# Moving the FFN units of a fused attention and FFN layer behind the output projection, and the weight build behind the first projections

## What is computed

```python
q = (x @ Wq + bq); k = (x @ Wk + bk); v = (x @ Wv + bv)     # 16, 2, 2 heads of 64
scores = einsum('bgrsd,bgswd->bgrsw', q, k_win)             # window of 256 keys around s
out = einsum('bgrsw,bgswd->bgrsd', softmax(scores), v_win)
x = layernorm(x + out @ Wo + bo)
W_real = unfold(G1_R, G2_R); W_imag = unfold(G1_I, G2_I)    # 512 x 512 each
xr, xi = split(x, 2)
y = layernorm(x + concat(xr @ W_real.T - xi @ W_imag.T + br,
                         xr @ W_imag.T + xi @ W_real.T + bi))
```

## Time and profile before

| | us |
|---|---|
| median of 3 runs | 1383.55 |
| lowest and highest of them | 1379.75, 1401.43 |
| the profiled execution | 1378.04 |
| its span on the slowest core (7) | 1376.5 |
| spans of all cores | 1366.8 to 1376.5 |

### The profile page before, as it was taken

How to read it: one execution, slowest core, us unless ns; L and a number is a source line. 1 busy time by engine, 2 the same in 40 slices (tenths; PEclk the granted TensorE clock), 3 DMA queues, 4 the chain that set the end, 5 groups by cost and what they waited for, 6 DMA issues and landing times.

```text
span 1376.5 us, 17007 instructions; the slowest of 8 cores (1366.8 to 1376.5 us)
## 1 busy us (share of the span) xinstructions
PE 808.0 (59%) x4568; PEld 357.5 (26%) x4568; DVE 553.9 (40%) x1539; ACT 396.1 (29%) x673; POOL 356.7 (26%) x324
## 2 busy tenths in 40 slices
PE   0033377665577666666665575666577558665654
PEld 0000132322233223332232232233232223222321
DVE  0044410355514551455554011455425541555553
ACT  3311134322333223332220234233232233332310
POOL 0000002443303340334330104433214430343410
PEclk9999987777677777877777686777687768877776
DMA  4500100000100001000000310000200020000000
GB/s 132 175 11 0 62 31 0 1 16 31 63 15 16 16 32 61 17 16 16 32 16 16 107 31 1 16 16 16 77 1 17 31 77 1 16 17 31 16 16 31
DMA packets 15869, 44.51 MB, mean 32 GB/s; under 512 B 3091, under 2 KB 5539, under 8 KB 15782
## 3 DMA queue, kind: packets, MB, share of 16 engines
q0 software_dynamic: 9216, 33.56, 6.7%
q1 hardware_dynamic: 6566, 9.87, 2.6%
HBM read 26.65 MB, written 16.78 MB: 32 GB/s over the span
## 4 chain that ended last, share of the span: by engine, by line
PE 53%; DVE 21%; issue 10%; DMA 7%; ACT 5%; POOL 1%; DVEq 1%; SPq 0%; ACTq 0%; POOLq 0%
PE pW L631 11%; PE pW L758 10%; PE pW L405 9%; PE pS L556 5%; DVE scr L644 5%; PE pS L499 4%; DVE attn L584 4%; DMA xs<-x 4%; PE pT L729 2%; PE pT L606 2%; DVE pre L777 2%; DVE x_tm L709 2%; PE pW L762 2%; DVE pre L674 1%; PE pW L635 1%
## 5 line engine op out<-in xcount | busy, mean ns | idle before, releaser
L517 ACT ACTIVATE EX<-pS,expbias 128x512 bf16<-128x512 f32 x384 | 242.7, 683 | 329.5 <-PE pS L499 329.1
L533 POOL TENSOR_TENSOR EX<-EX,maskr_s 128x512 bf16<-128x512 bf16 x128 | 172.1, 1368 | 276.0 <-ACT EX L517 275.4
L533 POOL TENSOR_TENSOR EX<-EX,maskl_s 128x512 bf16<-128x512 bf16 x128 | 148.5, 1181 | 323.7 <-ACT EX L517 323.7
L631 PE MATMUL pW<-wo_sb,attnT 128*128 128x512 bf16 x512 | 174.6, 502 | 35.3 <-DVE pre L777 33.8
L405 PE MATMUL pW<-XT,wq_sb 128*128 128x512 bf16 x512 | 127.8, 416 | 9.1 <-DVE XT L385 9.1
L729 PE MATMUL pT<-identb,x_tm 128*128 128x128 bf16 x256 | 32.3, 305 | 169.8 <-DVE x_tm L709 169.8
L644 DVE SCALAR_TENSOR_TENSOR scr<-pre 128x1024 bf16<-128x1024 f32 x64 | 120.5, 1883 | 6.7
L584 DVE TENSOR_SCALAR attn<-pS,Rrec 128x64 bf16<-128x64 f32 x512 | 110.2, 278 | 14.3 <-DVE attn L584 0.5
L499 PE MATMUL pS<-QT,KT 64*128 64x512 bf16 x384 | 101.9, 473 | 13.3 <-ACT EX L517 11.5
L574 DVE RECIPROCAL Rrec<-pS 128x4 f32<-128x4 f32 x128 | 23.3, 182 | 188.2 <-PE pS L556 187.9
L556 PE MATMUL pS<-VB,EX 128*128 128x65 bf16 x1536 | 89.6, 221 | 1.9 <-POOL EX L533 1.4
(11 more groups left out here) (81 smaller groups left out, 772.6 us busy)
## 6 DMA issues: line engine op xcount, KB each, us to landing
xs<-x POOLq DMA_DIRECT2D x32, 512.0 KB, 4.5
y<-outst POOLq DMA_DIRECT2D x32, 512.0 KB, 3.0
wstage<-wq SPq DMA_DIRECT2D x4, 512.0 KB, 4.0
xs<-wq SPq DMA_DIRECT2D x4, 512.0 KB, 4.3
wstage<-wo SPq DMA_DIRECT2D x4, 512.0 KB, 4.2
xs<-wo SPq DMA_DIRECT2D x4, 512.0 KB, 4.1
wstage<-wk SPq DMA_DIRECT2D x1, 512.0 KB, 4.4
xs<-wv SPq DMA_DIRECT2D x1, 512.0 KB, 4.5
```

Of the source, the lines that this page charges most:

```text
L517: i = sca.activation(EX[:, exi * 512:(exi + 1) * 512], pS[quad % 2][:, :], AF.Exp, bias=expbias[:])
L533: i = gps.tensor_mul(EX[:, exi * 512:(exi + 1) * 512], EX[:, exi * 512:(exi + 1) * 512], m[:]) \
L631: ten.matmul(pW[half][:, :], attnT[:, ring * 1024 + c * 128: ring * 1024 + (c + 1) * 128], wo_sb[:, c * 1024 + half * 512: c * 1024 + (hal ...
```

## The change

Two blocks are moved; no instruction is rewritten.

1. The building of the FFN matrices becomes a function `emit_wbuild`, called once, behind `emit_qkv(0, 0)` and `emit_qkv(0, 1)`, and it takes the state of pW0 and pW1 over from them.
2. In the loop, all of Q2's units stand together behind `wo_unit(P, 1)` and `ln1_unit(P)`, in front of `rstd1_unit(P)` and `x1norm_unit(P)`.

```diff
+        def emit_wbuild():
+            nonlocal ev_wrt, ev_wit
+            E.res("pW0b")["f"] = E.res("pW0")["f"]
+            E.res("pW1b")["f"] = E.res("pW1")["f"]
...
             emit_qkv(b, 0)
             emit_qkv(b, 1)
+            if b == 0:
+                emit_wbuild()
...
                 if S < 16:
                     sc_unit(b, S, 0, 0)
                     exp_unit(b, S, 0, 0)
-                if 0 <= Q2 < 16:
-                    x1t_unit(b, Q2)
                 if 0 <= P < 16:
                     av_unit(b, P, 0)
...
                 if 0 <= P < 16:
                     av_unit(b, P, 1)
-                if 0 <= Q2 < 16:
-                    ffn_unit(b, Q2, 0)
-                if 0 <= P < 16:
                     recip_unit(b, P, 0)
...
                 if 0 <= P < 16:
                     av_unit(b, P, 2)
-                if 0 <= Q2 < 16:
-                    ffn_unit(b, Q2, 1)
...
                     mask_unit(b, S, 2, 0)
-                if 0 <= Q2 < 16:
-                    ln2out_unit(b, Q2)
                 if 0 <= P < 16:
                     wo_unit(b, P, 0)
...
                 if 0 <= P < 16:
                     wo_unit(b, P, 1)
                     ln1_unit(b, P)
+                if 0 <= Q2 < 16:
+                    x1t_unit(b, Q2)
+                    ffn_unit(b, Q2, 0)
+                    ffn_unit(b, Q2, 1)
+                    ln2out_unit(b, Q2)
+                if 0 <= P < 16:
                     rstd1_unit(b, P)
                     x1norm_unit(b, P)
```

More of the change, by code:

```diff
@@ L266, in schedule @@
         ev_wrt = ev_wit = None
[L267 to L301, removed]
@@ L302, in schedule @@
+        def emit_wbuild():
+            nonlocal ev_wrt, ev_wit
+            E.res("pW0b")["f"] = E.res("pW0")["f"]
+            E.res("pW1b")["f"] = E.res("pW1")["f"]
+            for xi, (g1x, g2x, ev_gc) in enumerate([(g1b, g2b, ev_gconv1),
+                                                    (g1b2, g2b2, ev_gconv2)]):
+                for c in range(4):
                     if cur == "t":
-                        E.wait(ev_t1)
+                        if xi == 0 and c == 0:
+                            ten.wait_ge(SEMH["dc"], ev_g_r[1])
@@ L304, in schedule @@
                         E.wait(E.res("pW0b")["f"])
-                    i = ten.matmul(pW[0][:, :], d32[:, tt * 128:(tt + 1) * 128], t1s[:],
+                        E.wait(ev_gc)
+                    i = ten.matmul(pW[0][0:32, :], g1x[:, c * 32:(c + 1) * 32], r32[:],
                                    start=True, stop=True) if cur == "t" else None
[L307 to L318, removed]
@@ L319, in schedule @@
-                    if c != 0:
-                        E.inc("v", i if cur == "v" else None)
+                    ev = E.inc("t", i)
+                    if cur == "s":
+                        sca.wait_ge(SEMH["t"], ev[1])
+                        i = sca.copy(t1s[:], pW[0][0:32, :])
+                    ev_t1 = E.inc("s", i if cur == "s" else None)
+                    if cur == "t":
+                        E.wait(E.res("pW1b")["f"])
+                    i = ten.matmul(pW[1][0:16, :], g2x[:, c * 16:(c + 1) * 16], r16[:],
+                                   start=True, stop=True) if cur == "t" else None
@@ new lines, in emit_wbuild @@
+                    ev = E.inc("t", i)
+                    if cur == "s":
+                        sca.wait_ge(SEMH["t"], ev[1])
+                        i = sca.copy(t2s[:], pW[1][0:16, :])
+                    ev_t2 = E.inc("s", i if cur == "s" else None)
+                    if cur == "t":
+                        E.wait(ev_t2)
+                    i = ten.matmul(pW[1][:, :], d16[:], t2s[:], start=True, stop=True) \
+                        if cur == "t" else None
+                    ev = E.inc("t", i)
@@ new lines, in emit_wbuild @@
+                    if cur == "s":
+                        sca.wait_ge(SEMH["t"], ev[1])
+                        i = sca.copy(f2s[:], pW[1][:, :])
+                    ev_f2 = E.inc("s", i if cur == "s" else None)
+                    E.res("pW1b")["f"] = ev_f2
+                    for tt in range(4):
+                        if cur == "t":
+                            E.wait(ev_t1)
+                            E.wait(E.res("pW0b")["f"])
+                        i = ten.matmul(pW[0][:, :], d32[:, tt * 128:(tt + 1) * 128], t1s[:],
+                                       start=True, stop=True) if cur == "t" else None
+                        ev_f1 = E.inc("t", i)
@@ L321, in schedule @@
                         if cur == "v":
+                            vec.wait_ge(SEMH["t"], ev_f1[1])
+                            vec.wait_ge(SEMH["s"], ev_f2[1])
                             E.bar("v")
[L323 to L328, removed]
+                            if c == 0:
+                                i = vec.scalar_tensor_tensor(
+                                    wacc[:, tt * 512:(tt + 1) * 512], pW[0][:, :], 1.0,
+                                    f2s[:], ALU.mult, ALU.mult)
+                            else:
+                                i = vec.scalar_tensor_tensor(wtmp[:], pW[0][:, :], 1.0,
+                                                             f2s[:], ALU.mult, ALU.mult)
@@ new lines, in emit_wbuild @@
+                        if c != 0:
+                            E.inc("v", i if cur == "v" else None)
+                            if cur == "v":
+                                E.bar("v")
+                                i = vec.tensor_add(wacc[:, tt * 512:(tt + 1) * 512],
+                                                   wacc[:, tt * 512:(tt + 1) * 512], wtmp[:])
+                        ev_acc = E.inc("v", i if cur == "v" else None)
+                        E.res("pW0b")["f"] = ev_acc
+                if cur == "v":
+                    E.bar("v")
+                    if xi == 0:
+                        i = vec.tensor_copy(wrt[:], wacc[:])
+                    else:
+                        vec.tensor_copy(wit[:], wacc[:])
+                        i = vec.tensor_scalar(witn[:], wacc[:], -1.0, None, ALU.mult)
@@ L329, in schedule @@
+                ev = E.inc("v", i if cur == "v" else None)
                 if xi == 0:
-                    i = vec.tensor_copy(wrt[:], wacc[:])
+                    ev_wrt = ev
                 else:
[L332 to L346, removed]
+                    ev_wit = ev
+            E.res("pW0")["f"] = E.res("pW0b")["f"]
+            E.res("pW1")["f"] = E.res("pW1b")["f"]
+            if debug:
+                if cur == "g":
+                    gps.wait_ge(SEMH["v"], ev_wit[1])
+                    gps.dma_start(dbg["dwr"], wrt[:]).then_inc(SEMH["dc"], 16)
+                    gps.dma_start(dbg["dwi"], wit[:]).then_inc(SEMH["dc"], 16)
+                E.c["dc"] += 32
```

## The result

| | us |
|---|---|
| before, median of 10 runs | 1381.16 |
| after, median of 10 runs (1578.84 to 1583.53) | 1580.87 |
| ratio after to before | 1.144, 95% interval 1.142 to 1.147 |
| span of the profiled execution after, slowest core (3) | 1580.1 |

The kernel is 14% slower. The forecast was 1580, with a range of 1520 to 1620. The times given for runs are medians of all their executions, the ratios are of the executions in the chip's faster state alone; the few in the slower state move a median here by at most 1.6 us.

The account below looks back on a forecast made before the run. It took the kernel to be a chain of waits, TensorE busy 59%, with one layer norm exposed per step. Terms summing to +202 us on the profiled 1378.0 gave 1580 us, range 1520 to 1620.

Parts of the forecast that it names:

- 22 plain steps: Loop intervals from L606 to L606 holding an FFN, 11 per batch: 33.35 us each for 27.3, +133 in all.
- first interval: From k=1 to 2 in each batch, no FFN in it any more: 22.2 us for 25.72, -7 in all.
- into k=16: Interval into k=16 of each batch, where no exps are waited for: 30.9 us for 26.28, +9 in all.
- four projection steps: Intervals with a projection (k=5 and 9), x loads behind the output DMA: 75.5 us for 64.2, +45 in all.
- tails: Batch ends: a whole FFN and ln2 now stand before the last x1 transposes, +22 in all.
- weight build: FFN matrix building moved behind the first two projections: same instructions in series, taken as 0, bounds -4 and +3 us.
- Stretch 1: From w (start of last output-projection matmul) to next step's first exp: two layer norms exposed, 15.4 us for 5.45.
- Stretch 2: First exp to the attention transposes (L606, later L612): only scores, exps and AV left, 9.65 us for 13.1.
- Stretch 3: Attention transposes to w: wo half 0 no longer waits for ln2's first add, 8.3 us for 8.6.
- warm rival: TensorE stays warm through the new holes, FFN block costs 5.0 us instead of 6.9: 1523 us, 10%.
- contention rival: Last mask runs beside ln1's squares each time, w to copy 4.95 us, stretch 3 8.6: 1624 us, 7%.
- rival on the other side: L729's 169.8 us of waits go and ln2 costs nothing, first exp passing its activations: about 1208 us, 3%.

Follow-up runs that it names:

- e3: Changed kernel with both norms' small ScalarE activations, outst, output DMA and x1norm moved into the next step, behind exp (0,1) and first eight scalings: 1453.3 us.
- e5: Changed kernel with the first two x tile loads of the projections at k=5 and 9 issued in front of the output DMA: 1558.8 us.
- e2: Kernel before with only the weight build moved behind the first two projections: 1385.0 us, ratio 1.003.
- e4: Changed kernel with 12 extra, unread matmuls filling TensorE's hole in front of each FFN: 1522.8 us, ratio 1.102.
- e10: e7 with the four masks of chunk 0 issued behind exp (1,1) and waiting for it: 1199.5 us, ratio 0.868.
- e7: Changed kernel with Q2's norm and FFN units spread through the step, and early x loads at k=5 and 9: 1277.2 us, ratio 0.925.

## Why the prediction was right

The forecast was a sum of differences; here are its terms beside the ones measured. The measured ones come from the L606 and L612 rows of both batches of the two profiled executions and add up to the difference of the two spans, 1580.1 - 1376.5 = 203.6.

| term | forecast | measured |
|---|---|---|
| 22 plain steps | +133 (6.0 each) | +121 (5.5 each) |
| first interval, twice | -7 | -8 |
| into k=16, twice | +9 | +8 |
| four projection steps | +45 | +56 |
| tails, twice | +22 | +23 |
| weight build | 0 | +3 |
| sum | +202 | +203 |

That 1580 was met within 1 us owes something to two errors of 11 and 12 us that cancel.

**Stretch 1, w to the first exp.** Forecast 3.8 + 6.9 + 3.7 + 1.0 = 15.4. In the step shown: 3.72 (703.22 to 706.94), 7.63 (to 714.57), 3.73 (to 718.30), 0.97 (to 719.27), 16.05. That step has a slow FFN: over the 22 plain steps of the trace the FFN block takes 6.97 from the copy on and the stretch 15.5, so the 6.9 was right for the mean. Taking ln1 from the step without an FFN and the FFN block from the end of the batch was right, since these stretches already had the new order of things around them. e3 shows that the wait of 4.7 us behind the FFN is the queue's order and no dependence: with the order changed it is 0.86.

**Stretch 2, first exp to L612.** Forecast 9.65; 719.27 to 729.26 is 9.99, the longest of the 22, whose mean is 9.67. I had costed VectorE's late reciprocals at nothing, with 1 us as the bound, and on the mean they cost nothing.

**Stretch 3, L612 to w.** Forecast 8.3; 695.83 to 703.22 is 7.39, 729.26 to 737.00 is 7.74, and the mean of the 22 is 7.69. I took a value toward the 8.6 of the kernel before when k=1 of the second batch, the nearer row, had 7.8. This is the 0.5 us by which the plain step was sized too long.

**Projection steps.** The mechanism, x loads behind a DMA that waits for outst, was right: the load is issued 6.5 us behind the FFN (forecast 6.2), and e5 takes 22 us away with it. Its size was not: from issue to cast it is 6.6 us (400.15 to 406.79; 5.5 to 6.8 in the four steps), for the 4.64 of the earlier trace rows. The likely reason, which no run tests alone, is that the output DMA is now issued just in front of the load. And from that cast to the scores at 443.24 another 36.4, for 35.1. In the earlier trace rows the loads were issued almost 3 us behind the output DMA, and I carried their duration over to a place where its neighbour had changed.

**The weight build.** 0 forecast, +3 in the first steps of the profile, 1.003 in e2: within the bounds given.

**The rule and the rivals.** The warm rival (1523 us, 10%) did not come, but e4 made its case: with the hole filled the time is 1522.8. The FFN does take 5 us when warm, and filling the hole is worth 58 us. That is a version in which the hole is filled; in the changed kernel itself the FFN stayed at 6.9, as the sum had it. The Trainium skill (TensorE: Matmul & The Clock Gate, "HAM oscillation") says that waits between bursts of matmuls throttle the clock anew each time; the trace agrees, with 0.62 granted over the FFN behind a 3.7 us hole and 1.00 with the hole filled. The contention rival (squares beside masks, 1624 us) did not come either: after the change the squares take 1.23 us on the mean. The rival on the other side, no new wait in place of the old one, falls with the two wait rows above. Another order, though, reaches its 1208 and less (e10), with the rest of the step rearranged as well.

## What to carry to other kernels

Where a change moves a block, look in the old trace for places that already have the new neighbours, such as the first and last steps: durations copied from there held to a few tenths of a microsecond on the mean, while one copied from a place whose neighbour had changed was 2 us off in the step shown. In a kernel whose queues are written by hand, what stands behind a small waiting instruction decides: letting the exps and the x loads pass four activations of 0.2 to 0.3 us and what hangs on them gave back 127 us. And before trusting a clever order, look what GpSimd runs beside each VectorE instruction.

## What the runs showed of the hardware that I had not expected

VectorE's 128x1024 f32 to bf16 TENSOR_SCALAR, 0.81 us alone, did not take turns with GpSimd's masks. It started 1.03 us behind the start of the first of four masks of 1.1 us each, and ended 0.56 us behind the last one. In e7's trace this is so 22 times (3.7 to 4.3 us each, always ending some 0.56 us behind the last mask); the other ten take 0.81. The Trainium skill (SBUF — State Buffer, "SBUF: two separate sides") describes a port pair that VectorE and GpSimd share under an exclusive lock held for one whole instruction. The exclusion agrees with the trace. By that alone VectorE could have gone after the first mask; in these rows it had to wait for all four, which were queued without a gap.

It is not always so. In the kernel before, ln2's squares on VectorE do come between two masks, and GpSimd gives way:

```profile
567.68 1.27 ACT L517 ACTIVATE EX<-pS,expbias 128x512 bf16<-128x512 f32 x2 [2.62 <-PE pS L499]
...
568.51 3.24 POOL L533 TENSOR_TENSOR EX<-EX,maskr_s 128x512 bf16<-128x512 bf16 x2 [7.57 <-ACT EX L517]
...
569.38 1.37 DVE L644 SCALAR_TENSOR_TENSOR scr<-pre 128x1024 bf16<-128x1024 f32 x1
```

The two masks take 3.24 us together instead of 2.26, while ln1's squares of the same step (575.95, 2.38 us) end 1.09 us behind two masks that run from 574.98 to 577.24. In the first case the second exp ended at 568.95, behind the start of the first mask; in the other both exps had ended before the masks began. Whether this decides who waits, no run tests. The squares take 1.88 us on the mean in the kernel before, 1.23 after the change.

The changed kernel with useless matmuls in front of its FFNs was 4% faster, since the clock that was kept up is worth more than the work added: 12 matmuls in a 3.7 us hole gave back 1.8 us a block (58 us over 32).
